# Reordering the head of a fused Mamba-2 and expert-layer kernel: constants, first loads, weight split and two groups' squares

## The reference, cut to what matters

```
h  = rmsnorm(x, norm_mamba_w)                 # over 256 features
zxbcdt = h @ in_proj_w.T                      # 256 -> 1160: z 512, xBC 640, dt 8
xBC = silu(causal depthwise conv, 4 taps, + conv_b)
dt  = softplus(dt + dt_bias);  A = -exp(A_log)          # 8 heads
scan over the tokens: state = state*exp(dt*A) + dt*x*B;  y = C.state + D*x
y = rmsnorm(y * silu(z), ssm_norm_w) @ out_proj_w.T
h = y + x                                     # then a top-2 mixture of 8 experts
h = h + moe(rmsnorm(h, norm_moe_w), gate_w, w1, w2)
x = layernorm(x + h)
x = layernorm(x + ffn(x))                     # int8 weights, scaled
```

## Time and profile before

| what | us |
|---|---|
| median of the runs | 1236.36 |
| the profiled execution | 1236.05 |
| its span, first to last instruction | 1234.4 |
| TensorE busy | 1115.3 |
| VectorE busy | 686.6 |
| ScalarE busy | 620.6 |
| GpSimd busy | 372.8 |

### The profile page before, as it was taken

The page is one execution under the profiler, slowest core; times in us unless marked ns, Lnnn a source line. Parts: engine busy times, 40 slices in busy tenths (PEclk is TensorE's granted clock), DMA queues, the critical chain, the costliest instruction groups (busy, mean ns, idle before and its releaser), DMA issues. The chain is left out here.

```text
span 1234.4 us, 21831 instructions
## 1 busy us (share of the span) xinstructions
PE 1115.3 (90%) x7496; PEld 989.1 (80%) x7497; DVE 686.6 (56%) x1645; ACT 620.6 (50%) x1279; POOL 372.8 (30%) x328
## 2 busy tenths in 40 slices
PE   0799999999999999889999999999999936999996
PEld 0577777777777777779999999999999934888885
DVE  3567676767677767667432323323232326798875
ACT  1655656565655655345454444545444424465653
POOL 1213131515152525358404040403400037334200
PEclk9899999999999999999999999999999977999999
DMA  3020101111111101236331222313121123212101
GB/s 108 5 73 1 40 1 40 35 39 35 39 35 39 35 23 35 91 111 227 112 110 52 101 68 84 110 44 117 50 104 42 42 98 118 79 52 91 64 18 52
DMA packets 40386, 80.88 MB, mean 66 GB/s; under 512 B 6656, under 2 KB 30080, under 8 KB 39040
## 3 DMA queue, kind: packets, MB, share of 16 engines
q1 hardware_dynamic: 22816, 34.69, 8.5%
q0 software_dynamic: 7440, 35.66, 8.5%
q10 hardware_dynamic: 10064, 9.70, 2.3%
HBM read 48.31 MB, written 30.67 MB: 64 GB/s over the span
## 5 line engine op out<-in xcount | busy, mean ns | idle before, releaser
L1320 DVE TENSOR_TENSOR e_h_lo<-e_bank,e_h_hi 128x512 fp32r<-128x512 f32 x148 | 102.1, 691 | 287.8 <-ACT e_bank L641 285.4
L973 PE MATMUL e_bank<-e_x_hi,e_w_hi 128*128 128x256 f32 x592 | 170.0, 287 | 1.5 <-issue 1.3
L990 PE MATMUL e_bank<-e_w_hi,e_h_hi 128*128 128x256 f32 x592 | 170.8, 289 | 0.0
L974 PE MATMUL e_bank<-e_x_lo,e_w_hi 128*128 128x256 f32 x592 | 168.7, 285 | 0.0
L975 PE MATMUL e_bank<-e_x_hi,e_w_lo 128*128 128x256 f32 x592 | 168.7, 285 | 0.0
L992 PE MATMUL e_bank<-e_w_hi,e_h_lo 128*128 128x256 f32 x592 | 167.9, 284 | 0.0
L991 PE MATMUL e_bank<-e_w_lo,e_h_hi 128*128 128x256 f32 x592 | 167.8, 283 | 0.0
L639 ACT ACTIVATE e_h_hi<-e_bank 128x512 fp32r<-128x512 f32 x148 | 88.5, 598 | 78.7 <-PE e_bank L975 75.0
L1184 DVE SCALAR_TENSOR_TENSOR conv<-raw,conv_w,conv 128x512 f32<-128x512 f32 x120 | 96.2, 802 | 41.7 <-ACT conv L559 38.8
L973 PEld LDWEIGHTS e_bank<-e_x_hi,e_w_hi 128*128 128x128 f32 x592 | 114.7, 194 | 3.0 <-issue 3.0
L975 PEld LDWEIGHTS e_bank<-e_x_hi,e_w_lo 128*128 128x128 f32 x592 | 114.8, 194 | 0.0
(11 more groups left out here) (238 smaller groups left out, 2700.9 us busy)
## 6 DMA issues: line engine op xcount, KB each, us to landing
e_stage<-in_w POOLq DMA_DIRECT2D x9, 2048.0 KB, 8.4
e_x_rows<-sent_rows SPq DMA_DIRECT2D x38, 256.0 KB, 2.7
back_rows<-e_y_rows ACTq DMA_DIRECT2D x37, 256.0 KB, 2.2
x_in<-in_x SPq DMA_DIRECT2D x8, 512.0 KB, 4.2
x_res_dram<-x_res SPq DMA_DIRECT2D x8, 512.0 KB, 2.9
f_res<-x_res_dram SPq DMA_DIRECT2D x8, 512.0 KB, 3.8
out<-f_out_t SPq DMA_DIRECT2D x8, 512.0 KB, 2.6
back_rows<-zeros SPq DMA_DIRECT2D x8, 256.0 KB, 3.3
```

The lines of the kernel that those rows point to most:

```text
L973: mm(out, w1h[:, k, t], x_hi[:, k], start=k == 0, stop=False)
L974: mm(out, w1h[:, k, t], x_lo[:, k], start=False, stop=False)
L990: mm(out, eh_hi[:, k, t], w2h[:, k], start=k == 0, stop=False)
L1320: tt(flat(eh_lo[:, 2 * p:2 * p + 2]), h_ps[p][:], flat(eh_hi[:, 2 * p:2 * p + 2]).bitcast(F32), ALU.subtract).then_inc(es["h_lo_ready"], 1)
```

## The change

What it does, by engine:

- **Constants.** The separate block is gone. GpSimd makes the same constants at the top of the main block and signals `constants_ready`, for which TensorE waits; DVE's use of the identity is behind `iota_ready`, which comes later on GpSimd.
- **Loads.** SP issues x of group 0, `in_w`, `a_log` (one broadcast load of a row tiled four times on the host, counted on `a_in`), three loads counted on `conv_in`, x of group 1, six loads counted on `small_in` (`dt_bias` as one load, `w_out` the last), and x of group 2. Six DMAs fewer are issued.
- **VectorE.** It waits for `a_in`, makes the minimum, splits the weights' high parts, runs `moment(0)`, the first low part, `norm(0)`, the second low part, then negates. The eleven scaling instructions go into `scales()`, behind `h_parts(0)`.
- **ScalarE.** The activation table for exp and log is asked for at the top. The wait for `small_in` moves behind `h_parts(0)` and `squares(1)`; `h_parts(0)` waits for `conv_in`. `squares(1)` moves from w = 2 of group 0 to directly behind `h_parts(0)`, and writes its squares into a part of `xm`.

The diff, cut to its core:

```diff
-SMALL_DMAS = 8 + 2 * CH
+CONV_DMAS, SMALL_DMAS = 3, 6
...
             sp.dma_start(w_stage, io["in_w"]).then_inc(s["weights_in"], 16)
-            for dst, src in ((nm_w, "nm_w"), (conv_w, "conv_w"), (conv_b, "conv_b"), (d_col, "d_col"),
-                             (ssm_w, "ssm_w"), (moe_w, "moe_w"), (gate_w, "gate_w")):
+            sp.dma_start(a_log[:].rearrange("p c h -> p (c h)"), io["a_log"].partition_broadcast(P))\
+                .then_inc(s["a_in"], 16)
+            for dst, src in ((nm_w, "nm_w"), (conv_w, "conv_w"), (conv_b, "conv_b")):
+                sp.dma_start(dst[:], io[src]).then_inc(s["conv_in"], 16)
+            load(1)
+            sp.dma_start(dt_bias[:].rearrange("p c h -> p (c h)"), io["dt_bias"].partition_broadcast(P))\
+                .then_inc(s["small_in"], 16)
+            for dst, src in ((d_col, "d_col"), (ssm_w, "ssm_w"), (moe_w, "moe_w"), (gate_w, "gate_w"), (w_out, "out_w")):
                 sp.dma_start(dst[:], io[src]).then_inc(s["small_in"], 16)
-            for dst, src in ((dt_bias, "dt_bias"), (a_log, "a_log")):
-                for c in range(CH):
-                    sp.dma_start(dst[:, c, :], io[src].partition_broadcast(P)).then_inc(s["small_in"], 16)
-            sp.dma_start(w_out[:], io["out_w"]).then_inc(s["small_in"], 16)
-            load(1)
             load(2)
...
         @block.gpsimd
         def _(pool):
+            for n in ("ident", "le", "gt", "lt", "ones"):
+                i = nc.gpsimd.memset(cst[n][:], 0.0 if n == "ident" else 1.0)
+            i.then_inc(s["filled"], 1)
+            pool.wait_ge(s["filled"], 1)
...
+            nc.gpsimd.memset(zero1[:], 0.0)
+            nc.gpsimd.memset(zeros[:], 0.0)
+            nc.gpsimd.memset(half[:], -0.5).then_inc(s["constants_ready"], 1)
+            pool.wait_ge(s["constants_ready"], 1)
...
             def squares(g):
+                out = xm[:, 1] if g == 1 else x_norm
                 act.wait_ge(s[f"x_loaded{g % X_INS}"], 16 * (g // X_INS + 1))
                 wait(act, s["ms_ready"], g)
-                wait(act, s["ht_done"], KD * g)
+                if g != 1:
+                    wait(act, s["ht_done"], KD * g)
...
             def h_parts(g):
+                if g == 0:
+                    act.wait_ge(s["conv_in"], 16 * CONV_DMAS)
...
-            act.wait_ge(s["small_in"], 16 * SMALL_DMAS)
+            nc.scalar.preload_act_table_set("natural_log_exp_and_others")
             act.wait_ge(s["a_exp"], 1)
             nc.scalar.activation(a_neg[:], a_neg[:], ACT.Exp).then_inc(s["a_exp"], 1)
...
-                if w == 2 and 0 <= g + 1 < NG:
+                if w == 2 and 0 <= g + 1 < NG and g + 1 != 1:
                     squares(g + 1)
...
                     if 0 <= g + 1 < NG:
                         h_parts(g + 1)
+                    if g + 1 == 0:
+                        squares(1)
+                        act.wait_ge(s["small_in"], 16 * SMALL_DMAS)
...
             pe_passed = Pass(pe, es["pe_passed"])
+            pe.wait_ge(s["constants_ready"], 1)
...
             def norm(g):
                 dve.wait_ge(s["rs_ready"], g + 1)
+                if g == 1:
+                    dve.wait_ge(s["ht_done"], KD)
...
+            def scales():
+                dve.wait_ge(s["iota_ready"], 2)
+                dve.wait_ge(s["small_in"], 16 * SMALL_DMAS)
+                nc.vector.tensor_copy(run[:, 0, :], base_e[:]).then_inc(s["counts_link"], 1)
+                for k in range(KI):
+                    ts(w_out[:, k, :], w_out[:, k, :], ssm_w[:, k:k + 1], None, ALU.mult)
+                    ts(d_diag[:, k], ident[:], d_col[:, k:k + 1], None, ALU.mult)
...
+            dve.wait_ge(s["a_in"], 16)
+            ts(a_neg[:], a_log[:], A_LOG_MAX, None, ALU.min).then_inc(s["a_exp"], 1)
...
+            dve.wait_ge(s["weights_in"], 16)
+            for k in range(KD):
+                nc.vector.tensor_copy(w_hi[:, k], w_stage[:, k]).then_inc(s["w_split"], 1)
+            moment(0)
+            for k in range(KD):
+                if k == KD - 1:
+                    norm(0)
+                dve.wait_ge(s["w_split"], k + 1)
+                tt(w_lo[:, k], w_stage[:, k], w_hi[:, k].bitcast(F32), ALU.subtract)\
+                    .then_inc(s["w_split"], 1)
+            dve.wait_ge(s["a_exp"], 2)
+            ts(a_neg[:], a_neg[:], -1.0, None, ALU.mult).then_inc(s["a_ready"], 1)
...
                 if w == 0:
                     if ahead:
                         h_parts(g)
+                    if g == 0:
+                        scales()
```

More of the change, by code:

```diff
@@ L261, in mamba_and_experts @@
         s = {n: sem(n) for n in (
-            "weights_in", "small_in", "w_split", "w_scaled", "a_exp", "a_ready", "iota_ready", "sides_ready",
+            "filled", "constants_ready", "weights_in", "a_in", "conv_in", "small_in", "w_split", "w_scaled", "a_exp", "a_ready", "iota_ready", "sides_ready",
             "x_loaded0", "x_loaded1", "x_loaded2", "ss_ready", "ms_ready", "rs_ready", "xn_ready", "ht_done",
@@ L394, in _ @@
         def _(pool):
+            for n in ("ident", "le", "gt", "lt", "ones"):
+                i = nc.gpsimd.memset(cst[n][:], 0.0 if n == "ident" else 1.0)
+            i.then_inc(s["filled"], 1)
+            pool.wait_ge(s["filled"], 1)
+            for n, op, mult, step in (("ident", ALU.not_equal, 1, -1), ("le", ALU.is_ge, -1, 1),
+                                      ("gt", ALU.is_gt, 1, -1), ("lt", ALU.is_gt, -1, 1)):
+                m = cst[n][:]
+                nc.gpsimd.affine_select(out=m, in_=m, compare_op=op, fill=1.0 if n == "ident" else 0.0,
+                                        base=0, pattern=[[step, P]], channel_multiplier=mult)
+            nc.gpsimd.memset(zero1[:], 0.0)
+            nc.gpsimd.memset(zeros[:], 0.0)
+            nc.gpsimd.memset(half[:], -0.5).then_inc(s["constants_ready"], 1)
+            pool.wait_ge(s["constants_ready"], 1)
             nc.gpsimd.iota(iota_e[:], pattern=[[1, NE]], base=0, channel_multiplier=0,
@@ L515, in squares @@
             def squares(g):
+                out = xm[:, 1] if g == 1 else x_norm
                 act.wait_ge(s[f"x_loaded{g % X_INS}"], 16 * (g // X_INS + 1))
                 wait(act, s["ms_ready"], g)
-                wait(act, s["ht_done"], KD * g)
+                if g != 1:
+                    wait(act, s["ht_done"], KD * g)
                 for c in range(CH):
-                    nc.scalar.activation(x_norm[:, c], x_in[:, g % X_INS, c, :], ACT.Square,
+                    nc.scalar.activation(out[:, c], x_in[:, g % X_INS, c, :], ACT.Square,
                                          accum_out=stat[:, 0, c:c + 1]).then_inc(s["ss_ready"], 1)
             def h_parts(g):
+                if g == 0:
+                    act.wait_ge(s["conv_in"], 16 * CONV_DMAS)
                 for k in range(KD):
@@ L1101, in _ @@
             nc.vector.memset(side[:, NS:2 * NS], 1.0).then_inc(s["sides_ready"], 1)
[L1102 to L1122, removed]
             def moment(g):
@@ L1368, in ffn_weights @@
                 nc.vector.tensor_copy(ffn_w[:, t], w8[:, t]).then_inc(es["ffn_w_ready"], 1)
+            dve.wait_ge(s["a_in"], 16)
+            ts(a_neg[:], a_log[:], A_LOG_MAX, None, ALU.min).then_inc(s["a_exp"], 1)
+            w_stage = decay[:].rearrange("p a h t -> p (a h t)")[:, 0:KD * PROJ].rearrange("p (k n) -> p k n", k=KD)
+            dve.wait_ge(s["weights_in"], 16)
+            for k in range(KD):
+                nc.vector.tensor_copy(w_hi[:, k], w_stage[:, k]).then_inc(s["w_split"], 1)
+            moment(0)
+            for k in range(KD):
+                if k == KD - 1:
[5 more added lines that the diff above has]
+            ts(a_neg[:], a_neg[:], -1.0, None, ALU.mult).then_inc(s["a_ready"], 1)
+            dve.wait_ge(s["a_ready"], 1)
             links = {}
@@ L1388, in _ @@
                         convolve(g, 3)
-                    if 0 <= g + 1 < NG:
+                    if 1 <= g + 1 < NG:
                         moment(g + 1)
@@ L1828, in build @@
         }
[L1829 to L1847, removed]
         mamba_and_experts(nc, io, dram, cst, routing, sb)
@@ L1878 @@
         "moe_w": cols(arr("L0_attn_norm_moe_w"), KD),
-        "dt_bias": arr("L0_attn_dt_bias"),
-        "a_log": arr("L0_attn_A_log"),
+        "dt_bias": np.tile(arr("L0_attn_dt_bias"), CH),
+        "a_log": np.tile(arr("L0_attn_A_log"), CH),
         "w12": np.concatenate([w1, w2], axis=2),
```

2 lines of the change are left out of this document (added).

## The result

The changed kernel takes 1220.59 us in the median of four runs (1219.46 to 1227.09), beside 1235.84 for the kernel before (1233.69 to 1240.66): ratio 0.9882, 95% interval 0.9837 to 0.9928. The forecast was 1220.9. On another chip, with six runs of it and eleven of the kernel before, the ratio was 0.9884 (0.9847 to 0.9920).

The account below looks back on a forecast made before the run. The prediction took the serial head before the first projection matmul (31.23 us) as the bound. Gains of 13.8 there and 1.7 at w = 2 of group 0, 15.5 in all, gave a 1220.9 us median, range 1216 to 1226.5.

Parts of the forecast that it names:

- The start: Top of the kernel: without the constants' block, SP's first load is issued at 0.85 instead of 4.00, 3.15 us gained.
- The loads: Head: a_log lands at 7.9 and VectorE's minimum starts then, not at 18.85; 7.8 us from the load queue no longer awaited.
- From the minimum to the first tile: Head: first projection matmul 9.5 us after t, the minimum's start, where it was 12.4; first tile at 17.4.
- the upper end for the power: Head: GpSimd's power starts only after VectorE's first low part, so norm(0) at t + 4.7, not t + 3.6.
- Moved behind: After the first tile: scales() and squares(1) fit into idle time of VectorE and ScalarE and cost nothing, 2.2 us to spare.
- The second place: Group 0, w = 2: without squares(1) on ScalarE's chain, z_out and TensorE's third z tile come 1.7 us earlier.
- The sum: Whole kernel: 13.8 us from the head plus 1.7 from w = 2 of group 0 make 15.5.
- the 1.7 to within 3: Sign: distance from first tile to the end 1.7 us shorter, to within 3; otherwise the prediction is wrong.
- Rival 1: Group 0's z tiles: TensorE's clock no longer falls, 1.1 us more gained, 1219.8; chance 0.22 with its like.
- Rival 2: The head gives less: a_log lands at 8.8, SP starts late, or the clock falls elsewhere; 1221.8 to 1224.0; chance 0.20.
- rivals 3 and 5: 3: w = 2 of group 0 gives nothing, 1222.6, chance 0.06. 5: later stages swallow the gain, about 1236, 0.03.
- rival 4: ScalarE's moved wait for small_in: each microsecond w_out lands after 20.3 lengthens the path by one; slower past 35.8; chance 0.02.

Follow-up runs that it names:

- e1_block: Changed kernel with the constants made in a block of their own ahead of the main block again; 0.9902 of the kernel before.
- e4_power: Changed kernel with both low parts of the weights behind norm(0), VectorE idle during GpSimd's power; 0.9891 of the kernel before.
- e3_table: Changed kernel without the early request of ScalarE's activation table; 0.9896 of the kernel before.
- e5_after: The changed kernel itself, unaltered, run again on another chip; 1222.88 us beside 1236.53 for the kernel before, ratio 0.9884.
- e6_clock: Changed kernel with 15 unread matmuls filling TensorE's idle stretch before group 0's third z tile; 1220.25 us, 0.9863 of the kernel before.
- e7_x_first: Changed kernel with work needing only x (squares, moment, norm) ahead of the weights' split and the A_log minimum; 1222.91 us, 0.9890 of the kernel before.
- e10_broadcasts: Changed kernel with VectorE's minimum waiting for all small loads, and dt_bias and a_log as four loads each; 1231.65 us, 0.9941 of the kernel before.

## Why the prediction was right, step by step

- **The start.** Forecast 0.85, measured 0.96; 3.04 us gained in place of 3.15. The distance from the block to the main work is one to one (e1_block).
- **The loads.** a_log was put at 7.9 and landed just before 8.41, inside its bounds (7.3 to 8.8) but in their upper half. This is the term that was most mis-sized: 10.44 us gained at the minimum and not 10.9 (with the start's 0.1 in it). The composition, 3.63 for the count and 3.74 for the broadcasts, was not in the prediction, which had 7.8 for both.
- **From the minimum to the first tile.** Forecast 9.5, measured 9.32. The choice of the upper end for the power was right in size (norm(0) at t + 4.49, forecast 4.7) and in kind (e4_power). The page "SBUF — State Buffer" of the Trainium skill (§ SBUF: two separate sides) says that one of the two engines holds the shared ports for a whole instruction. The trace agrees but for 0.14 us: by that rule the power would have ended at 13.01, and it ended at 12.87, so some of GpSimd's 1.03 us lay beside VectorE's instruction. What released exp's table before the change was perhaps misread (e3_table leaves it open). The sum did not suffer, since in both readings the table is gone from the path. The forecast of 9.5 was met with an order that is not the best one: with VectorE idle beside the power it is 8.81 (e4_power).
- **Moved behind.** `scales()` and squares(1) cost nothing: the first `raw_out` is 2.99 behind the first tile, beside 2.94 before. The first convolution, at 22.20, is 4.47 behind it, beside 4.42.
- **The second place.** Forecast 1.7, measured 1.55 in the change and 1.59 when undone.
- **The sum.** 13.50 + 1.55 = 15.05 of the forecast 15.5. The span is 16.2 shorter; the rest, 1.1, comes between the z tiles and the experts and is less than two records of one kernel differ by there. From the first tile to the end the record is 2.7 us shorter than before (1200.5 and 1203.2), inside the 1.7 to within 3 that the prediction asked for; e5_after's, with 1204.9, would not have been. At equal mean clock the difference is 15.2 (1235.7 and 1220.5). So the mechanism and the size of the gain, 15 to 15.5, are borne out; that the median (1220.59) came within 0.3 us of the forecast is luck, with runs from 1219.46 to 1227.09.
- **Rival 1** did not come: the idle stretch of 4.0 us still brought the half clock. e6_clock shows its price (0.8 at that place) and that nothing of it is left 20 us further on. **Rival 2** came in its smallest part, a_log's landing at 8.4 (the start was on time), **rivals 3 and 5** did not come, and **rival 4** was far off, with 8 us of slack.

## What to carry to other kernels

In the head of a program, one semaphore that counts many loads makes the first instruction wait for the last load: count apart what is needed at different times, and order each engine's work by when its input lands, as e7_x_first did once more. A microsecond taken from a serial head comes through nearly whole here (15.2 us for the 15.05 of the start and the second place, 3.0 for the 3.5 of e7_x_first, and 7.1 left in e10_broadcasts where 7.8 was due, all at equal mean clock). But where the runs of one kernel on one chip lie 7 to 14 us apart, only the times of single instructions in the records, or many runs brought to equal clock, can show it. A wait moved down the stream is safe only with its slack measured: here 8 us, and 12 us of lateness would have cost nearly all the gain.

## What the runs showed of the hardware

- Two broadcast loads of 16 KB in place of eight of 4 KB let the 512 KB load behind them land 3.7 us sooner, with the same bytes. By their issue alone (six times 0.46 us) it would be 2.8. The eight loads are also more pieces (32 bytes a partition in place of 128), and no run tells the number of loads from the size of the pieces. The bytes are not the reason: while the small loads were in the queue, the DMA engines moved 4 GB/s.
- GpSimd's power on 128x4 takes 1.03 us alone and 2.07 beside a VectorE subtraction with both inputs in SBUF (1.36 us, itself not slowed).
- ScalarE makes the rounded copy of 128x1160 in 1.1 us a piece (2.23 for two), VectorE in 0.7 (1.43 for two), but ScalarE was idle there.
- A table load of ScalarE takes 1.28 us, with no other time lost ahead of it or behind it, also where ScalarE was at work just before: in the changed kernel tap ends at 23.93, the load runs from 23.94, and silu starts at 25.23.
- Behind idle stretches of 3.4 to 5.6 us ahead of the third z tile, TensorE's granted clock was at half for some of the z tiles in every record that was not filled. When it fell differs from record to record: in the changed kernel at about 35, 2 us into the idle stretch of 4.04, and in e7_x_first at about 34, half a microsecond after the tile had started, behind the same 4.04 (the tile's first matmul took 0.50 us there, and 0.79 in the changed kernel). Filled with 15 matmuls, those tiles ran at 1.00; in e6_clock the half clock came some 6 us after them.
- The first projection matmuls follow each other at 0.43 us (18.29 and 18.72 in the changed kernel), later ones at 0.23 (23.46 and 23.69), though the profile gives a granted clock of 1.00 for both.
